# Flamingo block on one Trainium2 core: key norms of the local attention spread over partitions through a DRAM buffer

## The chip, the core and the metric

The kernel runs on one core of a Trainium2 chip. The metric is the device time of one execution, in microseconds (us). Six instruction streams work side by side: TensorE (PE, its weight loads shown as PEld), VectorE (DVE), ScalarE (ACT), GpSimd (POOL) and SyncE (SP), which here issues nearly all transfers. The transfers of the core run on 16 DMA engines. The memory that the engines compute from has 128 partitions; DRAM (HBM) is outside. Engines wait for each other only through semaphores.

## The reference

Sixteen sequences of 256 tokens with 128 features go through one gated cross-attention to 1601 context tokens and then through a small transformer of 6 layers, each a local attention (16 heads of 64, windows of 32) and a gated feed-forward:

```python
def attn_layer(x, Wqkv, qs, ksc, Wo):
    q, k, v = split_heads(x @ Wqkv)
    q = l2norm(q) * qs
    k = l2norm(k) * ksc
    q = q * cos * scale + rotate_half(q) * sin * scale
    k = k * cos / scale + rotate_half(k) * sin / scale
    return local_attention(q, k, v) @ Wo
...
x = x + tanh(g_xattn) * cross_attention(layernorm(x), ctx, mask)
y = layernorm(x)
for i in range(6):
    y = attn_layer(shift_tokens(y), ...) + y
    y = ffn_layer(shift_tokens(y), ...) + y
x = x + tanh(g_ffn) * y
```

The change is about `l2norm(k)`: each key vector of 64 numbers is divided by its length.

## The kernel before

`cross_phase` computes the cross-attention (the first 2100 us or so), `ffn_phase` the 6 layers. Only `ffn_phase` is changed. It makes 6 x 16 = 96 passes, one for each layer and sequence ("block"). In the steady state one call of `iteration(A, B, C, D)` works on four blocks at once, each at another stage: A computes its queries, keys and values, B its scores and softmax, C its output projection, residual and layer norm, D the end of its feed-forward. An iteration has 8 steps (`k` = 0 to 7, STEPS), and the hardware loop holds two iterations in its body. Every engine has the order of its work written out by hand, and waits where it must.

Queries and keys stand transposed in `qT` and `kT`: 128 partitions are two heads of 64 dimensions, a free row is 256 tokens, and 8 such rows (NJ) hold the 16 heads. What matters here happens to block A:

- Steps 0 to 3: PE computes 8 groups of 512 columns into `b_qk` (first 4 for keys, last 4 for queries). DVE (`rotate`) multiplies each by the cosine table into `kT` or `qT` and by the sine table into `rot_s`. After each two groups SP swaps neighbouring partitions by two transfers `rot_p <- rot_s` (`swap(i)`, i = 0 to 3; 0 and 1 for keys, 2 and 3 for queries), and POOL adds them (`add_swapped(i)`, at steps 1 to 4).
- Step 2: PE sums the squares of the keys per head (`norms(0)`); the four groups land in partitions 0, 32, 64, 96 (even heads) and 1, 33, 65, 97 (odd heads) of `b_nv`. ACT turns them into 1/length (`inverse_norms(0)`, into `rn_k`), and POOL clamps them.
- SP then spreads the eight useful rows of `rn_k`, 512 numbers each, to 64 partitions apiece in `rkb`. SP's order is swap(0), swap(1), swap(2), the spreading, swap(3).
- Steps 4 and 5: POOL multiplies the keys by `rkb` (`scale_keys(0)` and `(1)`, each 4 of the 8 rows).

POOL has one more job in each step: it normalises the softmax rows of block B (`probs <- probs, rsums`, L1048). Its order is: at step 4 `probs` of one unit, `add_swapped(3)`, `scale_keys(0)`; at step 5 `probs` of the next unit, `scale_keys(1)`. PE transposes those `probs` (into `b_pt`, L1341) one step later.

Semaphores of this part: `rots_ready` (sine products done), `rnk_ready` (norms clamped), `kn_ready` (keys scaled), `rkb_in` (spreading landed), `swap0_in` and `swap1_in`. ACT writes `rn_k` of the next block only when the spreading of the last one is over.

Of the kernel before, what the change touches and what calls it, by code (L numbers as in the profile page):

```python
# [10 lines left out]
F32 = mybir.dt.float32  # L11
# [6 lines left out]
P = 128  # L18
S = 256
INNER, DH = 1024, 64  # L20
# [62 lines left out]
def wait_apart(eng, passed, sem, value):  # L83


    eng.wait_ge(sem, value)
    eng.sem_inc(passed, 1)
# [679 lines left out]
            rows(pe, iteration)  # L767


def ffn_phase(nc, xn_scr, x1_scr, ident, identb, ins, out, NB, DEPTH):  # L770
    with ExitStack() as ctx:
        def sb(name, shape, dt=F32):
            return ctx.enter_context(nc.sbuf_tensor(name, shape, dt))
# [1 line left out]
        def bank(name, n=1):  # L775
# [21 lines left out]
        rn_k = sb("rn_k", [P, 512])  # L797
# [26 lines left out]
        b_nv, b_pt, b_o, b_c = (bank(n) for n in ("b_nv", "b_pt", "b_o", "b_c"))  # L824

        per = dict(xs_ready=2, qk_done=8, sq_ready=8, rots_ready=8, rotc_ready=8, swap0_in=64, swap1_in=64,
                   norm_done=2, ln_ready=2, rn_ready=2, rnk_ready=1, rkb_in=128, rqt_done=1, rq_ready=2,
                   sum_ready=4, kn_ready=2, v_done=6, v_kept=6,
                   scores_done=8, max_ready=8, nb_ready=8, exp_ready=8, psum_ready=8, rsum_ready=8, pn_ready=8,
                   pt_done=8, pt_kept=8, o_done=8, o_kept=4, wo_done=2, x1_ready=1, xs1_ready=2, mu_done=1,  # L830
# [1 line left out]
                   h_done=3, h_kept=6, gelu_ready=1, hh_ready=1, w2_done=1, x_ready=1)  # L832
        owner = dict(xs_ready="pool", qk_done="pe", sq_ready="act", rots_ready="dve", rotc_ready="dve",
                     swap0_in="sp", swap1_in="sp", norm_done="pe", ln_ready="act", rn_ready="act", rnk_ready="pool",
                     rkb_in="sp", rqt_done="pe", rq_ready="dve", sum_ready="pool", kn_ready="pool",
                     v_done="pe", v_kept="act", scores_done="pe", max_ready="dve", nb_ready="dve", exp_ready="act",
                     psum_ready="dve", rsum_ready="dve", pn_ready="pool", pt_done="pe", pt_kept="act", o_done="pe",
                     o_kept="dve", wo_done="pe", x1_ready="dve", xs1_ready="pool", mu_done="pe", xc_ready="dve",
# [21 lines left out]
        def count(name, n, c, back=0):  # L860

            return n * per[name] + (AHEAD - back) * per[name] + c
# [44 lines left out]
        def _(sp):  # L907
# [35 lines left out]
            def iteration(A, B, C, D, begin=None):  # L943
                layer = here[0]

                def swap(i):
                    n = A[0]
                    wait_apart(sp, sp_passed, s["rots_ready"], count("rots_ready", n, 2 * i + 2))

                    wait_apart(sp, sp_passed, s["sum_ready"], count("sum_ready", n, i - 1))  # L950
                    for r in range(2):
                        sp.dma_start(rot_p[r:P:2, i % 2, :], rot_s[1 - r:P:2, i % 2, :]
                                     ).then_inc(s[f"swap{i % 2}_in"], 16)

                if A:
                    n = A[0]
                    swap(0)
                    swap(1)
                    swap(2)
                    wait_apart(sp, sp_passed, s["rnk_ready"], count("rnk_ready", n, 1))  # L960

                    wait_apart(sp, sp_passed, s["kn_ready"], count("kn_ready", n, 0))
                    for c in range(4):
                        for e in range(2):
                            src = rn_k[32 * c + e:32 * c + e + 1, :]
                            sp.dma_start(rkb[e * DH:(e + 1) * DH, c, :],
                                         src.unsqueeze(1).to_broadcast([1, DH, 512])
                                         ).then_inc(s["rkb_in"], 16)
                    swap(3)
                if begin is not None and not isinstance(layer, int):  # L970
                    last = layer * NB - 1
                    if begin == 1:
                        wait_apart(sp, sp_passed, s["wo_done"], count("wo_done", last, 2))
                        load(PART_O, layer)
                    if begin == 2:
                        wait_apart(sp, sp_passed, s["h_done"], count("h_done", last, 3))
                        load(PART_1, layer)
                        wait_apart(sp, sp_passed, s["x_ready"], count("x_ready", last, 1))
                        load(PART_2, layer)
                        load_vectors(layer)  # L980
# [9 lines left out]
        def _(pool):  # L990
# [20 lines left out]
            def iteration(A, B, C, D, begin=None):  # L1011
# [7 lines left out]

                def scale_keys(i):  # L1020
                    n, p = A[0], A[2]
                    pool.wait_ge(s["rkb_in"], count("rkb_in", n, 128))
                    pool.wait_ge(s["sum_ready"], count("sum_ready", n, i + 1))
                    dst = kT[:, p, 4 * i:4 * i + 4, :].rearrange("p j t -> p (j t)")
                    nc.gpsimd.tensor_tensor(dst, dst, rkb[:, 2 * i:2 * i + 2, :].rearrange("p c t -> p (c t)"), ALU.mult
                                            ).then_inc(s["kn_ready"], 1)
# [44 lines left out]
        def _(act):  # L1071
# [7 lines left out]
            def iteration(A, B, C, D, begin=None):  # L1079
                def inverse_norms(i, dst):  # L1080
# [5 lines left out]
                                         scale=LN_SCALE).then_inc(s["ln_ready"], 1)  # L1086
                    act.wait_ge(s["ln_ready"], count("ln_ready", n, i + 1))
                    if i == 0:
                        act.wait_ge(s["rkb_in"], count("rkb_in", n, 0))
                    else:  # L1090
                        act.wait_ge(s["rqt_done"], count("rqt_done", n, 0))
                    nc.scalar.activation(dst[:, :], ln_n2[:, :], ACT.Exp, bias=eps_c[:, 2:3],
# [367 lines left out]
def build(nc, ins, out, NB, DEPTH):  # L1460
    with ExitStack() as ctx:
        ident = ctx.enter_context(nc.sbuf_tensor("ident", [P, P], F32))
        identb = ctx.enter_context(nc.sbuf_tensor("identb", [P, P], BF16))
        x1_scr = nc.dram_tensor("x1_scr", [P, NB, S], F32, kind="Internal").ap()
        xn_scr = nc.dram_tensor("xn_scr", [P, NB, S], F32, kind="Internal").ap()
        ident_ready = ctx.enter_context(nc.semaphore("ident_ready"))
        with nc.Block() as block:
            @block.gpsimd
# [6 lines left out]
                                            pattern=[[-1, P]], channel_multiplier=1).then_inc(ident_ready, 1)  # L1475
                pool.wait_ge(ident_ready, 4)
        cross_phase(nc, x1_scr, xn_scr, ident, identb, ins, NB)
        ffn_phase(nc, xn_scr, x1_scr, ident, identb, ins, out, NB, DEPTH)

# [123 lines left out]
```

## Time and profile before

| | us |
|---|---|
| median of 3 runs | 10139.23 |
| lowest, highest | 10133.4, 10156.67 |
| the profiled execution, its own time | 10142.71 |
| its span in the profile | 10140.8 |

The span is cut into 40 slices in the profile, of 253.5 us each. All of `cross_phase` lies in the first 8.3 of them. The two phases differ in every row of the slices, so an average over the span says little about either. Times of day, such as 7085.06, are us from the start of the span. "Idle before, <-X" in a row is the time that the engine stood still just before this instruction, and whose signal ended it; SPq is SyncE's queue, whose durations are those of issuing a transfer, not of moving its bytes. "us to landing" is the time from issue to the completion signal.

### The profile page before, as it was taken

How to read it: one execution, taken by the hardware profiler on the slowest of the kernel's cores; microseconds unless marked ns; L12 is line 12 of the kernel's file. 1: busy time of each engine (PE TensorE's matmuls, PEld its weight loads, DVE VectorE, ACT ScalarE, POOL GpSimd, SP SyncE). 2: the span in 40 equal slices, each digit the busy share in tenths (PEclk: the TensorE clock that was granted, in tenths of full speed). 3: DMA queues.
4: the chain of work that ended last, by engine and by line, in shares of the span. 5: the costliest groups of instructions: out<-in, count | busy, mean ns of one | idle time of the engine just before them, and what ended most of it. 6: DMA issues, size and time to landing. Idle time of an engine off the chain costs nothing. (4 is left out here: it accounts for less than half of the span.)

```text
span 10140.8 us, 156224 instructions
## 1 busy us (share of the span) xinstructions
PE 6380.9 (63%) x50624; PEld 3634.1 (36%) x50624; DVE 4287.9 (42%) x9059; ACT 3885.0 (38%) x7910; POOL 2651.9 (26%) x2280
## 2 busy tenths in 40 slices
PE   7999999955555555555555555555555555555555
PEld 3444444423333333333333333333333333333333
DVE  5666666633333333333333333333333333333333
ACT  3555554533333333333333333333333333333333
POOL 2111111122222222222222222222222222322222
PEclk9999999977777777777777777777777777777777
DMA  3333333334444444444444444444444444444443
GB/s 71 64 64 64 66 63 63 64 55 39 39 39 38 45 45 38 38 38 45 43 39 38 40 46 46 39 39 39 39 48 41 38 40 39 47 40 38 38 38 42
DMA packets 175759, 465.91 MB, mean 46 GB/s; under 512 B 37356, under 2 KB 53612, under 8 KB 168732
## 3 DMA queue, kind: packets, MB, share of 16 engines
q1 hardware_dynamic: 173340, 453.94, 42.6%
q8 instruction: 530, 8.68, 0.4%
q14 instruction: 353, 2.89, 0.1%
q10 hardware_dynamic: 1536, 0.40, 0.0%
HBM read 122.55 MB, written 29.11 MB: 15 GB/s over the span
## 5 line engine op out<-in xcount | busy, mean ns | idle before, releaser
L1341 PE MATMUL b_pt<-ident,probs 128*128 128x128 f32 x3072 | 584.6, 320 | 2610.4 <-POOL probs L1048 2610.4
L1102 ACT ACTIVATE probsT<-b_pt 128x512 f32<-128x512 f32 x768 | 458.5, 597 | 3682.0 <-PE b_pt L1341 3680.5
L1178 DVE TENSOR_REDUCE psums<-probs 128x4 f32<-128x512 f32 (+1 forms) x768 | 469.6, 611 | 3212.9 <-ACT probs L1121 3103.4
L1121 ACT ACTIVATE probs<-b_sc,nb,rq 128x96 f32<-128x96 f32 (+1 forms) x3072 | 1110.8, 444 | 1037.5 <-DVE nb L1246 1036.8
L1341 PEld LDWEIGHTS b_pt<-ident,probs 128*128 128x128 f32 x3072 | 372.7, 157 | 2743.4 <-POOL probs L1048 2635.2
L1048 POOL TENSOR_TENSOR probs<-probs,rsums 128x512 f32<-128x512 f32 (+1 forms) x768 | 716.8, 933 | 2194.0 <-DVE rsums L1183 2192.9
L1017 POOL TENSOR_TENSOR qT<-qT,rot_p 128x1024 f32<-128x1024 f32 x192 | 450.5, 2346 | 3209.8 <-DMA rot_p<-rot_s 3209.8
L437 ACT ACTIVATE eT<-b_e 128x512 f32<-128x512 f32 (+1 forms) x1664 | 907.4, 594 | 977.1 <-PE b_e L755 971.9
L510 DVE CUSTOM_DVE_ANT_0 junk<-b_s,mq 128x1024 bf16<-128x1024 f32 (+1 forms) x1024 | 999.4, 990 | 456.9 <-PE b_s L737 413.4
L1208 DVE TENSOR_TENSOR rot_s<-b_qk,rot_tab 128x512 f32<-128x512 f32 x768 | 526.5, 686 | 763.4 <-ACT sq L1131 763.4
L1394 PE MATMUL b_qk<-xs,weights 128*128 128x256 f32 x3072 | 812.3, 402 | 44.2 <-POOL xs L1040 20.1
L1405 PE MATMUL b_qk<-weights,xs 128*128 128x512 f32 x1152 | 795.3, 822 | 45.8 <-ACT v L1143 21.6
L1321 PE MATMUL b_sc<-lmask,identb 128*128 128x256 bf16 (+1 forms) x1536 | 289.0, 272 | 638.0 <-ACT probs L1121 432.7
L751 PE MATMUL b_e<-mk,identb 128*128 128x512 bf16 (+1 forms) x1664 | 655.3, 394 | 40.2 <-DMA q_op<-mp 33.6
L755 PE MATMUL b_e<-q_op,k_op 75*128 75x256 bf16 (+1 forms) x3328 | 658.8, 280 | 0.0
L1394 PEld LDWEIGHTS b_qk<-xs,weights 128*128 128x128 f32 x3072 | 564.1, 199 | 193.1 <-DVE kT L1214 83.7
L1237 DVE TENSOR_REDUCE nmax<-b_sc 128x4 f32<-128x512 f32 (+1 forms) x768 | 474.0, 617 | 360.4 <-PE b_sc L1329 356.3
L1358 PE MATMUL b_o<-probsT,v 128*64 128x64 f32 (+1 forms) x9216 | 541.3, 256 | 80.2 <-ACT probsT L1102 80.2
L1358 PEld LDWEIGHTS b_o<-probsT,v 128*64 128x64 f32 x9216 | 396.4, 146 | 509.2 <-issue 415.7
L737 PE MATMUL b_s<-k_op,q_op 72*128 72x512 bf16 (+1 forms) x2048 | 516.9, 351 | 57.0 <-issue 43.5
L657 PE MATMUL b_pv<-eT,vx 128*9 128x256 f32 x6656 | 531.7, 392 | 3.9 <-ACT eT L437 3.9
L1329 PE MATMUL b_sc<-kT,qT 64*64 64x128 f32 (+1 forms) x12288 | 518.4, 288 | 11.2 <-issue 11.2
(128 smaller groups left out, 9157.9 us busy)
## 6 DMA issues: line engine op xcount, KB each, us to landing
rot_p<-rot_s SPq DMA_DIRECT2D x768, 256.0 KB, 2.4
rkb<-rn_k SPq DMA_DIRECT2D x768, 128.0 KB, 17.0
k_op<-k_scr SPq DMA_DIRECT2D x576, 100.1 KB
k_scr<-kp SPq DMA_DIRECT2D x48, 400.2 KB, 3.6
ctxT<-in_ctx SPq DMA_DIRECT2D x17, 800.5 KB, 18.6
weights<-in_ffn_w SPq DMA_DIRECT2D x24, 512.0 KB, 4.9
q_op<-q_scr SPq DMA_DIRECT2D x144, 64.0 KB
mt<-in_mask_k SPq DMA_DIRECT2D x17, 416.0 KB, 20.0
```

Source lines behind the costliest of these rows:

```text
L437: nc.scalar.activation(eT[0:n, g % 2, i * 512:(i + 1) * 512], b_e[i][0:n, :], ACT.Exp).then_inc(s["e_ready"], 1)
L510: nc.vector.tensor_tensor_reduce(junk[:, half, 0:n], b_s[u % 2][:, 0:n], mq[:, p, qt, half * 1024:half * 1024 + n], 1.0, LOWEST, ALU.add, ...
L657: last = nc.tensor.matmul(b_pv[32 * h:32 * h + DK + 1, 0:S], vx[0:n, p, kt, 4 * q + h, :], eT[0:n, g % 2, h * S:(h + 1) * S], start=(kt == ...
L751: nc.tensor.matmul(b_e[i][0:n, :], identb[0:n, 0:n], mk[0:n, p, kt, :].unsqueeze(1).to_broadcast([n, 2, S]), start=True, stop=False, skip_ ...
L755: last = nc.tensor.matmul(b_e[i][0:n, j * S:(j + 1) * S], k_op[q][0:MROW + 3, 2 * i + j, kt * P:kt * P + n], q_op[0:MROW + 3, p, 4 * q + 2 ...
L1048: nc.gpsimd.tensor_tensor(pu, pu, rsums[:, u % 2, :].unsqueeze(2).to_broadcast([P, 4, w]), ALU.mult).then_inc(s["pn_ready"], 1)
L1121: last = nc.scalar.activation(probs[:, t, k % 2, 2 * e + h, c0:P], b_sc[:, 512 * e + h * w:512 * e + (h + 1) * w], ACT.Exp, bias=nb[:, k % ...
L1208: nc.vector.tensor_tensor(per_block(rot_s[:, q % 2, 512 * (i % 2):512 * (i % 2 + 1)]), per_block(src), rot_tab[:, tab + 1, :].unsqueeze(1) ...
L1341: last = nc.tensor.transpose(b_pt[:, i * P:(i + 1) * P], probs[:, t, u % 2, i, :], ident[:, :])
L1358: last = nc.tensor.matmul(b_o[r, o0 + q0:o0 + q1], v[:, p, tile, vc], probsT[:, u % 2, c + q0:c + q1], start=True, stop=True, skip_group_c ...
L1394: last = nc.tensor.matmul(b_qk[:, 512 * (i % 2) + x * S:512 * (i % 2) + (x + 1) * S], weights[:, c0:c0 + P], xs[:, p, :], start=True, stop ...
L1405: nc.tensor.matmul(b_qk[:, 512 * e:512 * (e + 1)], xs[:, p, V0[k - 4]:V0[k - 4] + P], weights[:, W_V + e * 512:W_V + (e + 1) * 512], start ...
```

## The change

The eight transfers out of single partitions are replaced by two writes into a new DRAM buffer `rk_scr` of 2 x 4 x 512 numbers (one write for the even heads, from partitions 0, 32, 64, 96, one for the odd), a wait of SP for their landing, and two reads. Each read gives 64 partitions the same row of 2048 numbers, 8 KB. The bytes that arrive in `rkb` are the same 1 MB. ACT now waits for the writes (`rk_out`) before it overwrites `rn_k`, no longer for the spreading.

```diff
-                   norm_done=2, ln_ready=2, rn_ready=2, rnk_ready=1, rkb_in=128, rqt_done=1, rq_ready=2,
+                   norm_done=2, ln_ready=2, rn_ready=2, rnk_ready=1, rk_out=32, rkb_in=32, rqt_done=1, rq_ready=2,
...
                     wait_apart(sp, sp_passed, s["kn_ready"], count("kn_ready", n, 0))
-                    for c in range(4):
-                        for e in range(2):
-                            src = rn_k[32 * c + e:32 * c + e + 1, :]
-                            sp.dma_start(rkb[e * DH:(e + 1) * DH, c, :],
-                                         src.unsqueeze(1).to_broadcast([1, DH, 512])
-                                         ).then_inc(s["rkb_in"], 16)
+                    for e in range(2):
+                        sp.dma_start(rk_scr[e], rn_k[e:P:32, :]).then_inc(s["rk_out"], 16)
+                    wait_apart(sp, sp_passed, s["rk_out"], count("rk_out", n, 32))
+                    for e in range(2):
+                        src = rk_scr[e].rearrange("c t -> (c t)").unsqueeze(0)
+                        sp.dma_start(rkb[e * DH:(e + 1) * DH, :, :].rearrange("p c t -> p (c t)"),
+                                     src.to_broadcast([DH, 2048])).then_inc(s["rkb_in"], 16)
                     swap(3)
...
-                    pool.wait_ge(s["rkb_in"], count("rkb_in", n, 128))
+                    pool.wait_ge(s["rkb_in"], count("rkb_in", n, 32))
...
-                        act.wait_ge(s["rkb_in"], count("rkb_in", n, 0))
+                        act.wait_ge(s["rk_out"], count("rk_out", n, 0))
...
+        rk_scr = nc.dram_tensor("rk_scr", [2, 4, 512], F32, kind="Internal").ap()
```

No engine but SP has another order of instructions. SP's queue in the first iteration of the loop body, before, from swap(2) to swap(3) (L952 are the swaps, L966 is the spreading; L86 is a wait by itself):

```order
L952 DMA rot_p<-rot_s 64x1024 [waits sum_ready]
L952 DMA rot_p<-rot_s 64x1024
L86 REGISTER_ALU
L86 ISA [waits rnk_ready]
L966 DMA rkb<-rn_k 64x1x512 [waits kn_ready]
L966 DMA rkb<-rn_k 64x1x512 x7
L86 REGISTER_ALU
L86 REGISTER_ALU [waits rots_ready]
```

The same place after the change (L964 are the writes, L968 the reads):

```order
L952 DMA rot_p<-rot_s 64x1024
L86 REGISTER_ALU
L86 ISA [waits rnk_ready]
L964 DMA rk_scr<-rn_k 4x512 [waits kn_ready]
L964 DMA rk_scr<-rn_k 4x512
L86 ISA
L968 DMA rkb<-rk_scr 64x2048 [waits rk_out]
L968 DMA rkb<-rk_scr 64x2048
L86 REGISTER_ALU
L86 REGISTER_ALU [waits rots_ready]
```

Four transfers and one more wait stand where eight transfers stood; swap(3) stays behind them.

## Rows read from the trace of the kernel before

**Rows 1.** The page: span, and busy tenths of 40 slices with TensorE's clock.

```profile
span 10140.8 us, 156224 instructions
...
PE   7999999955555555555555555555555555555555
...
PEclk9999999977777777777777777777777777777777
```

**Rows 2.** Waits: engine line waited for, us in total, times, longest us.

```profile
POOL qT L1017 <- DMA rot_p<-rot_s: 3209.8, 192, 35.9
...
PE b_pt L1341 <- POOL probs L1048: 2610.4, 95, 30.7
```

**Rows 3.** The tile rkb: who waited (us, times), issue to landing.

```profile
  PE b_sc L1321: 31.1, 1
...
DMA to landing us min/median/max: 6.9/17.0/17.8
```

**Rows 4.** Timeline of one iteration, 7083 to 7131 us: start, duration, instruction, [idle before].

```profile
7083.61 1.10 SPq L952 DMA_DIRECT2D rot_p<-rot_s  x2
...
7085.06 26.61 SPq L966 DMA_DIRECT2D rkb<-rn_k  x8
...
7086.54 2.36 POOL L1017 TENSOR_TENSOR qT<-qT,rot_p 128x1024 f32<-128x1024 f32 x1 [0.64 <-DMA rot_p<-rot_s]
...
7089.18 0.68 DVE L1208 TENSOR_TENSOR rot_s<-b_qk,rot_tab 128x512 f32<-128x512 f32 x1
...
7091.35 1.04 POOL L1048 TENSOR_TENSOR probs<-probs,rsums 128x512 f32<-128x512 f32 x1 [1.55 <-DVE rsums L1183]
...
7102.36 0.92 PE L1329 MATMUL b_sc<-kT,qT 64*64 64x96 f32 x16
...
7111.99 9.34 SPq L952 DMA_DIRECT2D rot_p<-rot_s  x2
7124.86 2.34 POOL L1017 TENSOR_TENSOR qT<-qT,rot_p 128x1024 f32<-128x1024 f32 x1 [32.48 <-DMA rot_p<-rot_s]
7127.16 2.34 POOL L1025 TENSOR_TENSOR kT<-kT,rkb 128x1024 f32<-128x1024 f32 x1
7129.45 0.83 POOL L1048 TENSOR_TENSOR probs<-probs,rsums 128x384 f32<-128x384 f32 x1
```

**Rows 5.** The same timeline behind the wait, and the same matmuls elsewhere.

```profile
7095.91 1.99 PE L1405 MATMUL b_qk<-weights,xs 128*128 128x512 f32 x4 [0.47 <-ACT v L1143]
...
7130.34 1.12 PE L1341 MATMUL b_pt<-ident,probs 128*128 128x128 f32 x4 [27.05 <-POOL probs L1048]
...
7131.24 3.62 PE L1405 MATMUL b_qk<-weights,xs 128*128 128x512 f32 x4
...
7137.37 0.66 PE L1341 MATMUL b_pt<-ident,probs 128*128 128x128 f32 x4
```

**Rows 6.** Stretches: us, busy of five engines, clock, DMA engines' busy share, GB/s.

```profile
2105.00:2109.00 4.00, 0.00 (x0) 0.00 (x0) 0.00 (x0) 0.00 (x0) 0.29 (x1) 0.50 0.98 410
7017.40:7044.40 27.00, 0.05 (x4) 0.00 (x0) 1.64 (x6) 0.00 (x0) 5.43 (x4) 0.50 0.64 41
7089.00:7111.00 22.00, 10.87 (x80) 5.02 (x80) 8.61 (x23) 7.87 (x18) 1.66 (x3) 0.78 0.89 31
```

**Rows 7.** DMA issues: KB each, median us from issue to landing.

```profile
rot_p<-rot_s SPq DMA_DIRECT2D x768, 256.0 KB, 2.4
...
weights<-in_ffn_w SPq DMA_DIRECT2D x24, 512.0 KB, 4.9
...
x_scr<-y SPq DMA_DIRECT2D x16, 128.0 KB, 1.8
...
xT<-xn_scr SPq DMA_DIRECT2D x1, 2048.0 KB, 7.7
```

**Rows 8.** One iteration's busy times, in a stretch of 83.5 us (columns as above).

```profile
5000.00:5083.50 83.50, 47.95 (x398) 29.41 (x396) 33.23 (x74) 30.64 (x66) 24.48 (x20) 0.80 0.46 45
```

More of the change, by code:

```diff
@@ L767, in _, with ffn_phase @@
             rows(pe, iteration)
-def ffn_phase(nc, xn_scr, x1_scr, ident, identb, ins, out, NB, DEPTH):
+def ffn_phase(nc, xn_scr, x1_scr, rk_scr, ident, identb, ins, out, NB, DEPTH):
     with ExitStack() as ctx:
@@ L834, in ffn_phase @@
                      swap0_in="sp", swap1_in="sp", norm_done="pe", ln_ready="act", rn_ready="act", rnk_ready="pool",
-                     rkb_in="sp", rqt_done="pe", rq_ready="dve", sum_ready="pool", kn_ready="pool",
+                     rk_out="sp", rkb_in="sp", rqt_done="pe", rq_ready="dve", sum_ready="pool", kn_ready="pool",
                      v_done="pe", v_kept="act", scores_done="pe", max_ready="dve", nb_ready="dve", exp_ready="act",
@@ L1477, in build @@
         cross_phase(nc, x1_scr, xn_scr, ident, identb, ins, NB)
-        ffn_phase(nc, xn_scr, x1_scr, ident, identb, ins, out, NB, DEPTH)
+        ffn_phase(nc, xn_scr, x1_scr, rk_scr, ident, identb, ins, out, NB, DEPTH)
 def rotary_tables():
```

## The prediction

> **What bounds the kernel now.** I read the slices first. The kernel has two phases: in the first 8 slices PE is busy 9 tenths, from there on 5 tenths at a mean clock of 0.7 [rows 1]. The change touches only the second phase, 96 passes in which PE has nearly half of its time left over. So the question is what PE waits for there. The list of waits answers it: PE waited 95 times, 2610.4 us in all, for `probs` from POOL, and POOL waited 192 times, 3209.8 us in all, for a swap `rot_p<-rot_s` [rows 2]. Both belong to one event that comes once in an iteration.
>
> The timeline of one iteration shows it. Call t0 the moment at which SP begins to issue the spreading of the key norms, 7085.06. The eight issues take it 26.61 us, and only then can it issue swap(3), which takes another 9.34 us; the swap has landed at 7124.86, t0 + 39.8, when POOL goes on after 32.48 us of idling [rows 4]. Yet what swap(3) carries was ready long before: the last sine product ends at 7089.86, t0 + 4.8. POOL then does `add_swapped(3)`, `scale_keys(0)` and the softmax rows, and PE, which had finished its last scores at 7103.28 (t0 + 18.2), goes on at 7130.34 after 27.05 us of standing still [rows 4, 5]. ACT and DVE stand behind PE.
>
> Why does the spreading take so long? While it runs the 16 DMA engines are busy 89% of the time and move 31 GB/s [rows 6]. The same engines moved 410 GB/s at 98% when they read DRAM at the start of this phase [rows 6]. So their number is not the limit; all of them read one partition at a time, eight transfers of 128 KB out of one row of 2 KB each, 1 MB in all. A transfer lands 17.0 us after its issue [rows 3], while a swap of twice its size lands in 2.4 us [rows 7].
>
> **The change, part by part.** *Removed*: eight reads of a single partition. *Added*: two writes of 8 KB into DRAM, one wait, two reads of 512 KB out of DRAM. What counts is T, the time at which swap(3) has landed, because POOL's chain and then PE hang on it.
>
> How late may T be before PE notices? Behind T come 2.34 us, 2.34 us and 0.83 us of POOL's work, 5.5 us together [rows 4], and PE arrives at t0 + 18.2. So T may be t0 + 12.7.
>
> The writes. An issue takes 0.55 us (1.10 us for two [rows 4]), so the second is issued at t0 + 0.55. The nearest row for its landing is a store of 128 KB into DRAM, 1.8 us [rows 7]; ours is smaller, and I take the same: t0 + 2.4. SP waits there. Behind the wait in its queue stand the two reads and swap(3), and for swap(3) waits POOL; but swap(3) has no data before t0 + 4.8, so this wait alone holds nothing back.
>
> The reads are what the trace doesn't show: no transfer of before lets 16 engines read the same 8 KB of DRAM at once. From below: a read of 2048 KB out of DRAM landed in 7.7 us [rows 7], and at 410 GB/s its half is 2.6 us shorter, so 1 MB lands after 5.1 us, at t0 + 7.5. From above, while DRAM behaves as it does for other reads: two loads of 512 KB one after the other, 2 x 4.9 us [rows 7], t0 + 12.2. Far beyond that lies a DRAM that serves one region as slowly as the single partition is served, 31 GB/s; this is a rival below. I take 5.1 us, since xT's load is the nearest row: one transfer with long rows (16 KB a partition; ours have 8 KB).
>
> Swap(3) is issued at t0 + 4.8, waits behind the reads on the same DMA engines, and needs at most 2.9 us more (from 7083.61, its first issue, to POOL's start at 7086.54 [rows 4]): T = t0 + 10.4. The limit is 12.7. Hidden, with 2.3 us to spare. With the upper value T = t0 + 15.1, 2.4 us too late.
>
> So PE's wait goes away in full: 2610.4 us, and the first block's scores, which waited 31.1 us for scaled keys [rows 3], together 2641 us. Gains above that: while PE stands still, its clock is at 0.5 of full speed, 1.2 GHz [rows 6], and stays there for its first matmuls afterwards. Four transposes and the values' four matmuls take 1.12 and 3.62 us there, against 0.66 and 1.99 us for the same work at 2.4 GHz [rows 5]: 2.1 us an iteration. PE still idles for a few us for other reasons, and ACT's evictions lie between these matmuls, so I count a bit over a quarter: 0.6 x 96 = 58 us. In all 2700 us.
>
> What is late next? In 83.5 us PE was busy 47.95, DVE 33.23, ACT 30.64, POOL 24.48 us [rows 8]; part of PE's time was at the low clock. With 28 us less, an iteration takes some 55 us, so PE comes near to being full, but no engine is above it. Layer starts: SP loads weights behind swap(3), and since SP is free 30 us earlier there, they come earlier too. ACT's new wait for `rk_out` ends before the old one did. Both cost nothing.
>
> The sum: 10140.8 - 2641 - 58 = 7442 us of span, and 2 us around it. The median of the runs stands 3 us under the profiled execution; I forecast **7440 us**. The case's own range is from the full clock gain, 10140.8 - 2641 - 2.1 x 96 = 7298, to no clock gain with T 2.4 us late, 7500 + 230 = 7730.
>
> **The rivals.**
>
> *DRAM serves one small region slowly.* All 16 engines walk through the same 8 KB in step. For it: the single partition shows what happens when all sources are in one place, 31 GB/s against 410 [rows 6]. [...] Between the two rates I take the geometric middle, 113 GB/s: 1 MB then needs 9.3 us instead of 2.6 us, lands at t0 + 14.2, T = t0 + 17.1, 4.4 us over the limit, 4.4 x 96 = 422 us: **7860 us**. If it is 50 GB/s, 21 us, T is t0 + 28.8 and the time is about 8990 us; this tail I keep apart.
>
> This rival has a relative in the Trainium skill, "DMA: Bandwidth & Descriptors", section "Latency and other measured facts": copies whose rows per partition lie at large powers of two apart ran at 103 GB/s instead of 207, which it puts down, unverified, to streams in lock-step meeting on the same HBM channel. Rows at no distance at all are its extreme case. By that figure, an estimate, 1 MB would need 10.2 us, and the sum would be some 85 us above the rival's 7860. No run here shows it; the trace has only loads with distinct rows.
>
> *Slower than before.* The same mechanism at its end: if the region is served no faster than one partition (31 GB/s), 1 MB needs 33.8 us, lands 31.2 us later than in my forecast, and T = t0 + 41.6 against t0 + 39.8 before: the trip through DRAM comes on top, 1.8 x 96 = 173 us, **10310 us**. The point from which it decides is T = t0 + 39.8, a rate of 33 GB/s. I know no reason for DRAM to be that slow.
>
> *Another wait takes the place.* DVE, ACT and POOL have been caught up by PE's long wait in each iteration; without it, evictions or POOL's softmax rows may be late. For it: in the rest of the iteration PE, ACT and DVE hand work to each other and every one of them idles. Against it: steps ahead of the wait run now with nobody caught up, and POOL has over half of its time free [rows 8]. Price: if a third of the wait comes back, 9 x 96 = 864 us: **8300 us**.
>
> *The change doesn't do what it says*, because swap(3) is held up by something else: then the time stays. The data for it is there at t0 + 4.8 [rows 4], so this is out of the question unless the wait for the writes is very long.
>
> **How the numbers follow.** Forecast (7298 to 7730 us): 0.68. DRAM region slow to middling (around 7860, up to 8100): 0.13. Its tail up to 10100: 0.07. Another wait (8300): 0.06. Slower than before (10310): 0.03. Below 7298, since the clock stays high and loops tighten: 0.03. The range reaches from 7280, a little into the last case, to 7960, and holds the forecast and most of the second case, 0.8. A measurement of this kernel tells a difference of 0.2%, 20 us, from none. Faster: 0.96; within: 0.01; slower: 0.03.
>
> **What the profile after would show.** The wait of PE for `probs` falls from 27 us to under 1 us, and POOL's wait for swap(3) from 32 us to about 3 us (POOL's softmax rows before it end at t0 + 7.3 [rows 4], and T is t0 + 10.4). The reads land about 5 us after issue; over 8 us would put the first rival in its place, over 30 us the slower one. The DMA rate in the reads' stretch is above 200 GB/s. The clock in the slices of the second phase rises from 0.7 to 0.8 or 0.9, and PE's busy digit from 5 to 7 or 8. If an iteration takes 55 us and POOL's wait is gone, the working holds; if POOL's wait is gone and the iteration takes over 60 us, another wait has come, and the sum is wrong by it.

## The result

The changed kernel takes 7363.35 us (median of 4 runs, 7356.95 to 7374.43), the kernel before, timed beside it, 10136.31 us (10130.63 to 10156.67). The ratio is 0.7263, with a 95% interval of 0.7249 to 0.7277. The forecast was 7440 us, with a range from 7280 to 7960: the time lies in the range, 77 us under the forecast.

The page of the changed kernel, span, busy shares and slices; it answers to [rows 1]:

```profile
span 7358.9 us, 156029 instructions
...
PE 6187.5 (84%) x50624; PEld 3531.4 (48%) x50624; DVE 4429.1 (60%) x9059; ACT 3886.3 (53%) x7910; POOL 2661.5 (36%) x2280
...
PE   6999999999978888888888878888888888888777
...
PEclk9999999999989999999999999999999999999998
```

In the second phase (from slice 12 on) PE is busy 8 tenths in place of 5, and its clock is at 0.9 in place of 0.7. The list of waits (engine line waited for, us in total, times, longest) answers to [rows 2]:

```profile
POOL qT L1018 <- DMA rot_p<-rot_s: 458.5, 192, 7.0
```

POOL's wait for swaps fell from 3209.8 to 458.5 us. The wait of PE for `probs` from POOL, 2610.4 us before, has left the list; the page's row of these transposes (busy, mean ns, idle before them and what ended it) has 2.9 us of it. PE's wait for scaled keys, 31.1 us in one go before [rows 3], is 21.3 us in eight goes (us, times, in the second fence, out of the view of the tile `rkb`):

```profile
L1342 PE MATMUL b_pt<-ident,probs 128*128 128x128 f32 x3072 | 543.1, 303 | 3.1 <-POOL probs L1049 2.9
```

```profile
  PE b_sc L1322: 21.3, 8
```

The timeline of one iteration answers to [rows 4]; t0 is 5031.66 here:

```profile
5031.66 1.12 SPq L964 DMA_DIRECT2D rk_scr<-rn_k  x2
...
5034.02 1.12 SPq L968 DMA_DIRECT2D rkb<-rk_scr  x2
...
5036.69 1.14 SPq L952 DMA_DIRECT2D rot_p<-rot_s  x2
...
5042.47 2.35 POOL L1018 TENSOR_TENSOR qT<-qT,rot_p 128x1024 f32<-128x1024 f32 x1 [3.49 <-DMA rot_p<-rot_s]
...
5047.07 0.82 POOL L1049 TENSOR_TENSOR probs<-probs,rsums 128x384 f32<-128x384 f32 x1
...
5049.28 1.11 PE L1342 MATMUL b_pt<-ident,probs 128*128 128x128 f32 x4
...
5050.19 3.10 PE L1406 MATMUL b_qk<-weights,xs 128*128 128x512 f32 x4
```

The writes land and the reads are issued at t0 + 2.36, swap(3) is issued at t0 + 5.03 and has landed at t0 + 10.8. POOL's softmax rows end at 5047.89, 1.4 us ahead of PE, which comes without a wait. This iteration is better than most: over all of them T is t0 + 11.4 in the mean (10.5 to 12.5), the softmax rows end 1.0 us ahead of PE, and in 21 of 95 iterations they are less than 0.3 us ahead. The DMA issues, which answer to [rows 7]:

```profile
rot_p<-rot_s SPq DMA_DIRECT2D x768, 256.0 KB, 2.4
rkb<-rk_scr SPq DMA_DIRECT2D x192, 512.0 KB, 6.3
```

A read of 512 KB lands 6.3 us after its own issue, in the median. The forecast of 5.1 us was for both reads, from the issue of the first; counted so, the second has landed after 7.4 us in the mean, at t0 + 9.8.

### The profile page after: what moved, and what is told of

It reads as the page before. It is cut to its first block and busy times, and to the rows that moved or that the text cites. A ratio compares the mean times of both kernels' runs of the same rounds, so it can differ in the third digit from the quotient of the medians.

```text
span 7358.9 us, 156029 instructions
## 1 busy us (share of the span) xinstructions
PE 6187.5 (84%) x50624; PEld 3531.4 (48%) x50624; DVE 4429.1 (60%) x9059; ACT 3886.3 (53%) x7910; POOL 2661.5 (36%) x2280
## 5 line engine op out<-in xcount | busy, mean ns | idle before, releaser
L1103 ACT ACTIVATE probsT<-b_pt 128x512 f32<-128x512 f32 x768 | 458.5, 597 | 970.8 <-PE b_pt L1342 969.5
L1395 PE MATMUL b_qk<-xs,weights 128*128 128x256 f32 x3072 | 830.4, 409 | 44.4 <-POOL xs L1041 20.6
L1406 PE MATMUL b_qk<-weights,xs 128*128 128x512 f32 x1152 | 647.2, 677 | 74.9 <-ACT v L1144 38.3
L1018 POOL TENSOR_TENSOR qT<-qT,rot_p 128x1024 f32<-128x1024 f32 x192 | 451.8, 2353 | 458.5 <-DMA rot_p<-rot_s 458.5
L1359 PEld LDWEIGHTS b_o<-probsT,v 128*64 128x64 f32 x9216 | 375.8, 138 | 455.7 <-issue 329.5
L1359 PE MATMUL b_o<-probsT,v 128*64 128x64 f32 (+1 forms) x9216 | 518.7, 248 | 80.2 <-ACT probsT L1103 80.2
L1342 PE MATMUL b_pt<-ident,probs 128*128 128x128 f32 x3072 | 543.1, 303 | 3.1 <-POOL probs L1049 2.9
L1018 POOL TENSOR_TENSOR kT<-kT,rot_p 128x1024 f32<-128x1024 f32 x192 | 452.9, 2359 | 193.5 <-DMA rot_p<-rot_s 193.5
L1330 PE MATMUL b_sc<-kT,qT 64*64 64x128 f32 (+1 forms) x12288 | 502.8, 281 | 9.7 <-issue 9.7
```

The source lines that it names most:

```text
L1018: nc.gpsimd.tensor_tensor(dst, dst, rot_p[:, i % 2, :].rearrange("p (j t) -> p j t", j=4), ALU.add).then_inc(s["sum_ready"], 1)
L1342: last = nc.tensor.transpose(b_pt[:, i * P:(i + 1) * P], probs[:, t, u % 2, i, :], ident[:, :])
L1359: last = nc.tensor.matmul(b_o[r, o0 + q0:o0 + q1], v[:, p, tile, vc], probsT[:, u % 2, c + q0:c + q1], start=True, stop=True, skip_group_c ...
L1395: last = nc.tensor.matmul(b_qk[:, 512 * (i % 2) + x * S:512 * (i % 2) + (x + 1) * S], weights[:, c0:c0 + P], xs[:, p, :], start=True, stop ...
L1406: nc.tensor.matmul(b_qk[:, 512 * e:512 * (e + 1)], xs[:, p, V0[k - 4]:V0[k - 4] + P], weights[:, W_V + e * 512:W_V + (e + 1) * 512], start ...
```

## Why the spreading was slow

Two readings of the 40 us are possible: **A**, sixteen DMA engines read one partition at a time, and **B**, eight transfers with rows of 2 KB are slow wherever they read. A third, **C**, holds that only the place of swap(3) in the queue costs time. Throughout, the kernel before was timed beside each run: 10164.2 us beside the two runs that change the source and the destination of the reads, 10150.4 beside the last two runs, 10152.8 beside all others. Where it takes 10152.8, a ratio of 0.7263 is 7374 us.

**Distinct partitions.** The kernel before, with a source row per destination row:

```diff
-                            src = rn_k[32 * c + e:32 * c + e + 1, :]
-                            sp.dma_start(rkb[e * DH:(e + 1) * DH, c, :],
-                                         src.unsqueeze(1).to_broadcast([1, DH, 512])
+                            sp.dma_start(rkb[e * DH:(e + 1) * DH, c, :],
+                                         rot_tab[e * DH:(e + 1) * DH, 2:4, :].rearrange("p a t -> p (a t)")
                                          ).then_inc(s["rkb_in"], 16)
```

> The kernel before, with its eight transfers of 64 rows of 2 KB as they were, but each row now comes out of a partition of its own (rows of the rotary table stand in for the key norms, so the keys are scaled by wrong numbers). Theory A (sixteen DMA engines reading one partition is what was slow): the eight transfers take little more than their issue, 8 x 0.55 = 4.4 us, swap(3) lands at about t0 + 8, PE no longer waits, and the time is that of the changed kernel, 7360 us within 40. Rival B (eight transfers of 2 KB rows are slow, wherever they read): landing 17 us, swap(3) at t0 + 40, time 10140 us. A result between the two would share the cost between them.

Measured: 7354.28 us, ratio 0.7244 (0.7223 to 0.7265). The issues of this kernel:

```profile
rkb<-rot_tab SPq DMA_DIRECT2D x768, 128.0 KB, 2.4
```

The same eight transfers, of the same bytes and rows, land 2.4 us after issue in place of 17.0, and the whole gain is there without DRAM. B falls, A stands: it was that all bytes of a transfer came out of one place. Whether that place is the partition or something that several partitions share, no run was made for, but the trace of the kernel before has a hint (columns as in [rows 6]):

```profile
7104.00:7108.00 4.00, 0.00 (x0) 0.00 (x0) 1.02 (x5) 0.00 (x0) 0.00 (x0) 0.50 0.85 41
7108.00:7112.00 4.00, 0.00 (x0) 0.00 (x0) 0.00 (x0) 0.00 (x0) 0.00 (x0) 0.50 0.91 28
```

In the four stretches of 4 us ahead of these the rate is 28, 27, 27 and 32 GB/s, while the source goes on through partitions 0, 1, 32, 33; it rises to 41 about where it goes over from 33 to 64, the fourth transfer to the fifth. So partitions 0, 1, 32 and 33 seem to share one limit, and 64 to have another.

**Swap(3) first.** The kernel before, with one call moved.

```diff
                     swap(2)
+                    swap(3)
                     wait_apart(sp, sp_passed, s["rnk_ready"], count("rnk_ready", n, 1))
...
-                    swap(3)
```

> The kernel before, with one change of order: swap(3) is issued ahead of the eight transfers. Rival C (only the place of swap(3) behind the spreading costs time): swap(3) lands at t0 + 8, POOL's wait for it is gone, the time falls to near 7400 us. Theory A with the chain as read in the prediction: the spreading itself must land before scale_keys(0), which stands ahead of the softmax rows on POOL. It starts 5.9 us later and ends at about t0 + 5.9 + 37 = t0 + 43; then 2.3 + 0.8 us of POOL instead of 5.5 us, so PE goes on at t0 + 46.1 instead of t0 + 45.3: 10140 + 80 = 10200 us, and the wait in the list changes its name from the swap to the spreading.

Measured: 10372.85 us, ratio 1.0218 (1.0186 to 1.0249). The list of waits:

```profile
POOL kT L1025 <- DMA rkb<-rn_k: 3283.5, 96, 34.9
...
PE b_pt L1341 <- POOL probs L1048: 2855.8, 95, 33.1
```

C falls: the wait is as long as before and has another name. The loss is 220 us, where 80 were expected, so the expectation had the size wrong; counted from the clamp of the norms, POOL starts `scale_keys(0)` 2.5 us later than in the kernel before, in the mean, where I had put 0.8, and PE's waits add up to 245 us more than before. Why the spreading is ready later there was not found out.

**DRAM, but rows of 2 KB.** (The diffs from here on leave out the counts of `rkb_in`, which follow the number of transfers.)

```diff
-                    for e in range(2):
-                        src = rk_scr[e].rearrange("c t -> (c t)").unsqueeze(0)
-                        sp.dma_start(rkb[e * DH:(e + 1) * DH, :, :].rearrange("p c t -> p (c t)"),
-                                     src.to_broadcast([DH, 2048])).then_inc(s["rkb_in"], 16)
+                    for c in range(4):
+                        for e in range(2):
+                            sp.dma_start(rkb[e * DH:(e + 1) * DH, c, :],
+                                         rk_scr[e, c].unsqueeze(0).to_broadcast([DH, 512])
+                                         ).then_inc(s["rkb_in"], 16)
```

> The changed kernel, but the norms are read from DRAM in eight transfers of 64 rows of 2 KB in place of two of 64 rows of 8 KB. Theory A: the source is DRAM, so it is fast whatever the rows; six more issues of 0.55 us delay swap(3)'s issue to t0 + 2.4 + 4.4 = t0 + 6.8, the engines are busy with 1 MB until about t0 + 8.5, T is t0 + 11 to 12, within the slack of 12.7: 7363 us within 40. Rival B (2 KB rows and eight transfers are the slow thing): most of the time comes back, over 9000 us.

Measured: 7427.27 us, ratio 0.7316 (0.7295 to 0.7337), 53 us above the changed kernel's ratio. The rows of 8 KB are therefore a small part of the change: they save six issues. POOL's waits for swap(3) are longer by 88 us than in the changed kernel (546.4 against 458.5), and in 29 iterations PE waits for it again, 19.6 us in all. I had expected the cover to hold within 40 us; it is thinner than I read it.

## What the reads from DRAM cost, and why

The prediction took 5.1 us to landing and named one danger, all engines reading the same 8 KB of DRAM (**H**). The stretch in which the reads run moves 216 GB/s with the engines fully busy, half of the 410 of [rows 6] (columns as there):

```profile
5036.50:5039.50 3.00, 2.93 (x18) 0.80 (x18) 2.56 (x6) 0.34 (x2) 1.04 (x1) 1.00 1.02 216
```

The rate varies: over all iterations it lies between 180 and 290 GB/s from one us to the next while the reads run. The rival explanation is the destination, 64 partitions in a block (**D**). Two kernels tell them apart. In the first the source differs:

```diff
-                        src = rk_scr[e].rearrange("c t -> (c t)").unsqueeze(0)
...
-                                     src.to_broadcast([DH, 2048])).then_inc(s["rkb_in"], 16)
+                                     ins["ffn_w"][0, e * DH:(e + 1) * DH, 0:2048]).then_inc(s["rkb_in"], 16)
```

> The changed kernel, but the two reads take 64 rows that differ (out of the weights in DRAM, so the keys are scaled by wrong numbers) in place of 64 times the same 8 KB. It asks why the reads land 6.3 us after issue and run at 204 GB/s, when xT's load ran at 410. Theory H (sixteen engines on the same 8 KB of DRAM hinder each other): landing falls to about 5.1 us, the rate rises to 400 GB/s. Theory D (the destination limits: 64 partitions in a block take half of what 128 take): landing stays at 6.3 us and the rate near 204 GB/s. The time stays at 7363 us within 20 under both, since T is within its slack.

In the second the destination does:

```diff
-                        src = rk_scr[e].rearrange("c t -> (c t)").unsqueeze(0)
-                        sp.dma_start(rkb[e * DH:(e + 1) * DH, :, :].rearrange("p c t -> p (c t)"),
-                                     src.to_broadcast([DH, 2048])).then_inc(s["rkb_in"], 16)
+                        src = rk_scr[e].rearrange("c t -> (c t)").unsqueeze(0)[:, 0:1024]
+                        sp.dma_start(rkb[:, 2 * e:2 * e + 2, :].rearrange("p c t -> p (c t)"),
+                                     src.to_broadcast([P, 1024])).then_inc(s["rkb_in"], 16)
```

> The changed kernel, but each of the two reads writes 128 partitions with the same 4 KB, in place of 64 partitions with the same 8 KB (as many bytes; the keys are scaled by numbers of the wrong head). Theory D (destination of 64 partitions in a block limits): the rate rises from 204 to about 400 GB/s, landing falls from 6.3 to about 4.5 us. Theory H (the shared source in DRAM limits): the source is now only 4 KB, so no faster: landing 6.3 us or more, rate 204 GB/s or less. The time stays at 7363 us within 20 under both.

Measured: 7388.73 us (0.7268, 0.7245 to 0.7291) and 7358.85 us (0.7239, 0.7218 to 0.7260); neither can be told from the changed kernel. What counts are the landings, of the first and then of the second:

```profile
rkb<-in_ffn_w SPq DMA_DIRECT2D x192, 512.0 KB, 6.6
```

```profile
rkb<-rk_scr SPq DMA_DIRECT2D x192, 512.0 KB, 4.7
```

And the stretch of the reads in the second:

```profile
5029.00:5031.00 2.00, 1.93 (x4) 0.56 (x4) 1.97 (x5) 0.21 (x1) 0.40 (x2) 1.00 0.95 313
```

Sixty-four different rows of DRAM are no faster than 64 times the same (6.6 against 6.3 us), so H falls. With 128 partitions as destination as many bytes land in 4.7 us and run at 313 GB/s, so D stands, though the 400 GB/s that I had expected were not reached, and what takes the rest is open. The second kernel also halves the rows to 4 KB; that this made it fast is not likely, since xT's load has rows of 16 KB and is the one that ran at 410 GB/s. The run out of distinct partitions moves 216 GB/s too (from 5028 to 5033 us), but it reads as well as writes blocks of 64, so it does not tell source from destination. The Trainium skill, "SBUF — State Buffer", section "Door 1: The DMA port swizzle", says that DMA bandwidth goes by how many of 16 ports a transfer's partitions reach, that partitions 0 to 63 reach half of them, and gives 435 GB/s for all. Half is 218, and 216 was measured in the stretch shown; one port would be 27, and the kernel before moved 27 to 32 in most stretches of 4 us and 31 over all 22 us [rows 6]. For the first the trace agrees; for the second it lies a little above. Of the Trainium skill's row-pitch figure, which the prediction weighed against the change, nothing was seen for rows at no distance (6.3 against 6.6 us).

**One read in place of two.** This one asks what the shape of the source does.

```diff
-                    for e in range(2):
-                        src = rk_scr[e].rearrange("c t -> (c t)").unsqueeze(0)
-                        sp.dma_start(rkb[e * DH:(e + 1) * DH, :, :].rearrange("p c t -> p (c t)"),
-                                     src.to_broadcast([DH, 2048])).then_inc(s["rkb_in"], 16)
+                    src = rk_scr.rearrange("e c t -> e (c t)").unsqueeze(1)
+                    sp.dma_start(rkb[:, :, :].rearrange("p c t -> p (c t)"),
+                                 src.to_broadcast([2, DH, 2048])).then_inc(s["rkb_in"], 16)
```

> The changed kernel, with one read of 1 MB (2 heads x 64 partitions x 8 KB) in place of two of 512 KB. If only the bytes matter: landing and T as before or 0.5 us earlier, 7363 us within 20. Rival: the Trainium skill, DMA: Bandwidth & Descriptors, section on why a DMA increments its semaphore by 16, says that the engines used are the largest number up to 16 that divides the slowest dimension on both sides; the source's slowest dimension is now 2. Two engines, at the 25 GB/s that each of sixteen had in the fast stretch (410 GB/s in all), need 21 us: landing 24 us after issue, T about t0 + 10 if swap(3) passes on the other engines but its last descriptors wait on those two, so T about t0 + 27, 14 us late, 7363 + 14 x 96 = 8700 us.

Measured: 8926.29 us, ratio 0.8793 (0.8767 to 0.8818). Two stretches during the read, the second without most of swap(3), and POOL's wait for swap(3) in the same iteration (t0 is 5005.46):

```profile
5011.00:5029.00 18.00, 9.11 (x78) 4.40 (x78) 6.85 (x20) 7.30 (x17) 1.04 (x1) 0.89 0.19 77
5014.00:5026.00 12.00, 6.11 (x60) 3.31 (x58) 4.97 (x15) 6.28 (x15) 0.00 (x0) 0.95 0.12 52
```

```profile
5032.24 2.34 POOL L1017 TENSOR_TENSOR qT<-qT,rot_p 128x1024 f32<-128x1024 f32 x1 [19.38 <-DMA rot_p<-rot_s]
```

The engines are busy 19% in the mean of the first stretch, which has swap(3)'s share of all sixteen in it, and 12% in the second; two of sixteen would be 12.5%, and 52 GB/s are 26 for each of two. Swap(3) has landed at t0 + 26.8, where the expectation had t0 + 27 for two engines; the rule of the Trainium skill that it names (the number of engines divides the outermost dimension) agrees. That the read is one transfer of 1 MB is not the cause: xT's load is one of 2 MB and lands in 7.7 us [rows 7]. The outer dimension of 2 in the source makes the change lose more than half of its gain.

## How the time follows T

The prediction made everything of T, the landing of swap(3), with a slack up to t0 + 12.7. To move T, transfers of the old kind (128 KB out of one partition, into a tile that nobody reads) were put between the reads and swap(3): 1, 3 and 6 of them; the diff is that of three. They count into `rkb_in`, so `scale_keys` waits for them too, and so does ACT before it overwrites `rn_k`.

```diff
+                    for c in range(3):
+                        src = rn_k[32 * (c % 4):32 * (c % 4) + 1, :]
+                        sp.dma_start(rkx[0:DH, c, :], src.unsqueeze(1).to_broadcast([1, DH, 512])
+                                     ).then_inc(s["rkb_in"], 16)
                     swap(3)
...
-                        act.wait_ge(s["rk_out"], count("rk_out", n, 0))
+                        act.wait_ge(s["rkb_in"], count("rkb_in", n, 0))
```

> The changed kernel plus one transfer of the old kind (128 KB out of one partition, into a tile that nobody reads) between the reads and swap(3). Theory T (the time is set by when swap(3) has landed, with a slack up to t0 + 12.7): an old transfer takes about 4.1 us of the queue, T goes from t0 + 11.4 (mean of the changed kernel) to t0 + 15.5, 2.8 us over the slack, 7363 + 2.8 x 96 = 7632 us. Rival (a delay is not hidden at all): 7363 + 4.1 x 96 = 7757 us. Rival (slack far larger than read): 7363 us.

> As the run with one extra transfer, with three. Theory T: T = t0 + 23.7, 11.0 us over the slack, 7363 + 1056 = 8419 us; if TensorE's clock also falls for good behind a wait of this length, up to 1.5 us more in each of 96 iterations, 8560 us.

> As the run with one extra transfer, with six. Theory T: T = t0 + 36.0, 23.3 us over the slack, 7363 + 2237 = 9600 us without any loss by the clock; with 1.5 us of slow matmuls behind the wait in each iteration 9744 us. The line through the kernel before (T = t0 + 40.0, 10136 us) with one us for one us gives 10136 - 4.0 x 96 = 9752 us. So a value near 9750 says that the clock is a step that comes with a long wait, one near 9600 that the kernel before lost something else.

Measured: 7439.74 us (0.7325, 0.7312 to 0.7337), 8190.15 us (0.8063, 0.8047 to 0.8079) and 9131.86 us (0.8990, 0.8972 to 0.9008). All three are under what theory T expected. The lists of waits, of one, three and six extra transfers, show which of its parts was off:

```profile
POOL qT L1023 <- DMA rot_p<-rot_s: 556.3, 192, 8.0
...
PE b_pt L1347 <- POOL probs L1054: 20.6, 33, 3.0
```

```profile
POOL qT L1023 <- DMA rot_p<-rot_s: 1243.6, 192, 15.5
...
PE b_pt L1347 <- POOL probs L1054: 672.9, 95, 10.2
```

```profile
POOL qT L1023 <- DMA rot_p<-rot_s: 2200.5, 192, 25.2
...
PE b_pt L1347 <- POOL probs L1054: 1613.3, 95, 20.5
```

The price of a transfer was off: the first moves T by (556.3 - 458.5) / 96 = 1.0 us, probably because it runs while swap(3) would wait for its issue and for the reads anyway (no run shows this apart); each further one moves it by 3.3 to 3.6 us, not 4.1. The law itself holds. From three to six, POOL's waits grow by 957 us and the time by 942 us: one us of T is one us of every iteration.

Now take from each time that of the changed kernel (7374 us) and the growth of PE's waits for `probs` and for scaled keys, of which the changed kernel has 2.9 and 21.3 us. What remains is 816 - 661 = 155 us for three, 1758 - 1611 = 147 us for six, 1552 - 1396 = 156 us for the one read, and for the kernel before 2779 - 2617 = 162 us, each good to some 20 us. It is nearly the same for PE waits of 7, 17, 15 and 27 us: a sum that comes once with a wait and doesn't grow with it. With one extra transfer PE waits in only 33 iterations and with rows of 2 KB in 29, and the remainder is 57 and 38 us. This is the term that the prediction called the clock's and took at 58 us.

**Swap(3) ahead of the writes and reads**, in the changed kernel, asks whether any slack is used up.

```diff
                     swap(2)
+                    swap(3)
                     wait_apart(sp, sp_passed, s["rnk_ready"], count("rnk_ready", n, 1))
...
-                    swap(3)
```

> The changed kernel, with swap(3) issued ahead of the two writes and two reads. Swap(3) then lands at t0 + 8, the norms at t0 + 5.9 + 2.4 + 6.3 = t0 + 14.6; POOL starts scale_keys(0) there and has the softmax rows at t0 + 17.8, where PE comes for them at t0 + 18.2. Theory T with this chain: no difference, 7363 us within 20. If the slack were already used up in the changed kernel, one of the two orders must be visibly faster, by over 40 us.

Measured: 7619.78 us, ratio 0.7497 (0.7484 to 0.7509). My expectation was wrong by 246 us. Waits, and the place in the timeline (t0 is 1.1 to 1.6 us behind the start of the norms' clamp in the other kernels, and so 5016.7 to 5017.2 here):

```profile
POOL kT L1026 <- DMA rkb<-rk_scr: 509.7, 96, 6.5
...
PE b_pt L1342 <- POOL probs L1049: 132.5, 95, 4.3
```

```profile
5033.42 2.35 POOL L1026 TENSOR_TENSOR kT<-kT,rkb 128x1024 f32<-128x1024 f32 x1 [6.31 <-DMA rkb<-rk_scr]
...
5036.86 1.12 PE L1342 MATMUL b_pt<-ident,probs 128*128 128x128 f32 x4 [1.96 <-POOL probs L1049]
...
5037.77 2.96 PE L1406 MATMUL b_qk<-weights,xs 128*128 128x512 f32 x4
```

The norms are there at t0 + 16.2 or later, not at 14.6: I had counted 6.3 us for both reads, and they take 7.1 here from the first issue to the second landing. PE waits 1.4 us in each iteration, 132.5 us in all, and the time grows by nearly twice that: 246 us, less the growth of PE's two waits, 113, leave 133 us. So the remainder comes with a wait of 1.4 us already.

Behind the wait the four transposes take 1.12 us here and the values' four matmuls 2.96, against 0.66 and 1.99 at 2.4 GHz [rows 5]. A single iteration proves nothing, though: in the changed kernel's iteration shown above they took 1.11 and 3.10 without any wait. Counted over all iterations, at this place (behind the softmax rows that follow `scale_keys(0)`):

| kernel (all in us) | PE's wait each | four transposes, mean | values' four, mean | iterations with values over 2.5 | both, more than changed kernel, x96 | remainder |
|---|---|---|---|---|---|---|
| changed | 0 | 0.85 | 2.40 | 39% | | |
| swap(3) ahead | 1.4 | 1.08 | 3.40 | all | 118 | 133 |
| three extra | 7.1 | 1.11 | 3.46 | all | 127 | 155 |
| one read | 14.7 | 1.11 | 3.40 | all | 122 | 156 |
| six extra | 17.0 | 1.11 | 3.37 | all | 118 | 147 |
| before | 27.5 | 1.11 | 3.55 | all | 136 | 162 |

The eight matmuls behind the wait account for 78 to 89% of the remainder. What a wait of any of these lengths does is to make them slow in every iteration and not in four of ten.

**Swap(3) between the writes and the wait for them** tells whether that order costs by itself.

```diff
                         sp.dma_start(rk_scr[e], rn_k[e:P:32, :]).then_inc(s["rk_out"], 16)
+                    swap(3)
                     wait_apart(sp, sp_passed, s["rk_out"], count("rk_out", n, 32))
...
-                    swap(3)
```

> The changed kernel, with swap(3) between the two writes and SP's wait for them. It tells apart two readings of the run with swap(3) ahead of everything, which took 7620 us where no difference was expected. Reading 1 (POOL's chain was late there: scale_keys(0) started at t0 + 16.1 and the softmax rows came 1.1 us after PE): here the reads are issued by t0 + 6.7 and land at t0 + 13, scale_keys(0) starts no later than t0 + 13.3, the rows come at t0 + 16.5, before PE at t0 + 18.2: no wait, 7355 to 7365 us. Reading 2 (swap(3) ahead of the reads costs something by itself, such as the norms missing at scale_keys(0)): again over 7500 us.

Measured: 7376.87 us, ratio 0.7250 (0.7224 to 0.7276), the same as the changed kernel. The order is free as long as the softmax rows come ahead of PE. It is no better either.

**PE kept busy in the wait.** The last one takes on the remainder itself, in the kernel before. (PE's wait for a free `b_pt`, `pt_kept`, is moved ahead of the useless matmuls.)

```diff
+                    if A and B and u == 4:
+                        for _ in range(25):
+                            nc.tensor.matmul(b_pt[:, :], mean_mat[:, :],
+                                             rot_raw[:, 0:2, :].rearrange("p a t -> p (a t)"),
+                                             start=True, stop=True)
                     pe.wait_ge(s["pn_ready"], count("pn_ready", n, u + 1))
```

> The kernel before, in which PE does 25 useless matmuls (512 columns of constants into b_pt, which is free then) during its long wait in each iteration; the results are the same. They take some 26 us of the 27.5 us that PE waits. Theory of the clock (of what the change gained, 1.4 to 1.7 us an iteration are not the wait but matmuls at 1.2 GHz behind it): the granted clock of the span rises from 0.81 to over 0.9, the values' matmuls behind the wait fall from 3.6 to 2.0 us, and the time falls by 1 to 1.6 us in each of 96 iterations, 100 to 150 us, to about 10000 us. Rival (the 1.5 us are something else, such as the engines starting up behind the wait one after the other): no difference within 20 us, or slower if the extra matmuls outlast the wait.

Measured: 10125.19 us (median of 10 runs, 10094.25 to 10142.77), ratio 0.9976 (0.9966 to 0.9986): 24 us faster, a fifth of what was expected. The useless matmuls take 23 us of each wait, and the granted clock of the span rises from 0.81 to 0.93. Yet 434.3 us of waiting are left (4.6 us each), and behind that rest many of the matmuls are slow again: at the place of the table the transposes take 1.00 us and the values 3.08 us in the mean, these over 2.5 us in 79% of the iterations. The mean duration of a matmul of the values says it (line, count, busy, mean ns; the kernel before, then with PE kept busy, then the changed kernel):

```profile
L1405 PE MATMUL b_qk<-weights,xs 128*128 128x512 f32 x1152 | 795.3, 822 | 45.8 <-ACT v L1143 21.6 <-DVE qT L1214 19.0
```

```profile
L1409 PE MATMUL b_qk<-weights,xs 128*128 128x512 f32 x1152 | 760.1, 791 | 48.0 <-DVE qT L1214 24.3 <-ACT v L1143 19.9
```

```profile
L1406 PE MATMUL b_qk<-weights,xs 128*128 128x512 f32 x1152 | 647.2, 677 | 74.9 <-ACT v L1144 38.3 <-DVE qT L1215 30.5
```

The edit recovered 35 us of these matmuls' busy time and 24 us of time; the change recovers 148 us of theirs and 162 us beyond PE's waits. Both pairs are alike in size, and the table says the same for five kernels: the remainder is for the most part the clock. It was reasoned from traces, not by a run that changes the clock alone; a run in which the clock stays high through the wait, which would show it outright, was not had.

## Why the prediction was right, point by point

- **What bounds the kernel**: right. One event an iteration, the spreading ahead of swap(3) in SP's queue; the run out of distinct partitions shows as its cause that each transfer reads one partition, and the run with swap(3) first shows that it is the spreading and not the order.
- **Writes and wait**: 2.4 us forecast, 2.36 measured. Nothing was held up by them.
- **The reads**: 5.1 us forecast for both, 7.4 measured (upper bound 9.8). The step that was off is the nearest row: xT's load writes 128 partitions, these write 64. Swap(3) then needed 1.6 us behind them and not the 2.9 of the forecast, so T came out at t0 + 11.4 in the mean (10.8 in the iteration shown) for 10.4. That two errors offset each other here was luck.
- **The slack**: PE comes at t0 + 17.6 in the iteration shown, 0.6 us earlier than read. The spare 2.3 us were 1.4 us there and 1.0 us in the mean; T about 1 us later (rows of 2 KB, one extra transfer: 12.3) already costs 53 and 66 us. The wait is hidden, but only just.
- **The wait**: 2641 us forecast, gone but for 24: 2.9 us for `probs`, and 21.3 of the 31.1 us for scaled keys, which the prediction took to go as well.
- **The clock**: the mis-sized term. I counted a bit over a quarter of 2.1 us, 58 us in all, since PE idles elsewhere too; 2782 us of span less the 2617 of waits that went are 165 us, 1.7 us an iteration. The 107 us more, less the 24 us of waits that stayed, are the 83 us by which the span is under the forecast's 7442. The eight matmuls that I priced became faster by 1.4 us an iteration, two thirds of the 2.1: they are still slow in four iterations of ten, where my quarter had them slow in seven. The bound of the case, 7298 us, had room for it.
- **The rivals**: DRAM slow for one small region, and slower than before as its end, did not happen (6.6 us with distinct rows). Another wait did not come: PE is the busiest engine at 84%, and POOL's, ACT's and DVE's waits that are left stood there before. The iteration was forecast at some 55 us and takes 53.6 us in the mean.

## What to carry to other kernels

A broadcast out of one partition was by far the slowest source here: 31 GB/s with all DMA engines busy, and it held the queue for all that stood behind it. Take a trip through DRAM (2.4 us here for the write) or any source spread over partitions, keep the outermost dimension of the source large (64 was fast, 2 lost over half of the gain, nothing between was run), and let the destination span all 128 partitions if the landing counts. A wait of TensorE that is removed was worth more than its length, by 1.4 to 1.7 us each here; one that comes back in every iteration, of 1.4 us or of 17, costs that much again. And read the slack from all iterations, not from one: the one shown had 1.4 us, the mean 1.0, and a fifth of them next to nothing.

## What the runs showed of the hardware

- 1 MB out of one partition at a time: 31 GB/s with the engines 89% busy (27 to 32 in most stretches of 4 us, 41 where the source goes from partition 33 to 64); the same transfers out of 64 partitions land in 2.4 us in place of 17.0.
- Reads of one 8 KB region of DRAM by 16 engines: no slower than reads of 64 different rows, 6.3 against 6.6 us.
- A destination of 64 partitions in a block: 216 GB/s in a stretch of 3 us; of 128 partitions: 313 GB/s in one of 2 us, both from DRAM.
- An outer dimension of 2: the engines 12% busy at 52 GB/s, and swap(3) landed at t0 + 26.8, 16 us later than with two transfers whose outer dimension is 64.
- PE waits of 1.4 us and of 27 us alike leave 133 to 162 us behind them over 96 iterations. 118 to 136 us of it are eight matmuls behind the wait that run slow each time.
